# Recurrent layers on one core: Pool's B products in pairs of 1024 columns in a ring of eight, C products split as before, the gated y written in place

## What is computed

```python
xc, z = split(x @ in_w.T)                      # 512 inner channels each
u  = silu(causal_conv4(xc) + cb)
dt, Bm, Cm = split(u @ xp_w.T)                 # rank 16, state 16, state 16
dt = softplus(dt @ dt_w.T + dt_b)
A  = -exp(A_log)
def step(h, inp):                              # over tokens
    dt_t, B_t, C_t, u_t = inp
    h = exp(dt_t[:, :, None] * A) * h + (dt_t * u_t)[:, :, None] * B_t[:, None, :]
    y = einsum('bdn,bn->bd', h, C_t)
y = (ys + u * Dskip) * silu(z)
h = layer_norm(y @ out_w.T) ; x = h + residual
```

## Time and profile before

| what | value |
|---|---|
| median of 3 runs | 9465.37 us (9464.44 to 9467.9) |
| profiled execution, its own time | 9470.18 us |
| span of that execution, first to last instruction | 9468.5 us |
| mean granted PE clock | 0.949 of full speed |
| busy, share of the span | PE 87%, PEld 50%, DVE 88%, ACT 60%, POOL 54% |
| first scan, last scan (their starts) | 4538.3 us, 8777.1 us |

### The profile page before, as it was taken

How to read it: one execution, slowest core, us unless ns; L and a number is a source line. 1 busy time by engine, 2 the same in 40 slices (tenths; PEclk the granted TensorE clock), 3 DMA queues, 4 the chain that set the end, 5 groups by cost and what they waited for, 6 DMA issues and landing times. The chain is left out here.

```text
span 9468.5 us, 173659 instructions
## 1 busy us (share of the span) xinstructions
PE 8233.9 (87%) x48392; PEld 4721.2 (50%) x48392; DVE 8331.3 (88%) x12866; ACT 5642.4 (60%) x9235; POOL 5082.2 (54%) x4769
## 2 busy tenths in 40 slices
PE   6699999999999997897888888887788888888699
PEld 2366666666666666564333333333233333333466
DVE  5788888888888887997899999999699999999899
ACT  2377777777777775332666666665456656555333
POOL 1100000000000000785899999999699999999687
PEclk8799999999999999998999999999899999998899
DMA  7988888888888888111122111221222222211111
GB/s 236 306 272 281 282 280 283 281 281 279 282 283 281 280 280 267 46 43 47 77 82 82 72 56 77 82 82 44 94 80 72 76 91 91 91 68 71 53 43 40
DMA packets 1173912, 1447.40 MB, mean 153 GB/s; under 512 B 83402, under 2 KB 1053658, under 8 KB 1140736
## 3 DMA queue, kind: packets, MB, share of 16 engines
q1 hardware_dynamic: 1173568, 1444.18, 46.3%
HBM read 880.81 MB, written 564.60 MB: 153 GB/s over the span
## 5 line engine op out<-in xcount | busy, mean ns | idle before, releaser
L2109 POOL TENSOR_TENSOR mb_bx<-mb_dtu,mb_bc 128x512 f32<-128x512 f32 x2048 | 2662.0, 1324 | 13.7 <-DVE mb_hs L2209 13.2
L2352 PE MATMUL mb_y_ps<-mb_g,ident 128*128 128x512 f32 x4096 | 2187.1, 640 | 469.2 <-POOL mb_g L2116 235.0
L2396 ACT ACTIVATE mb_dA<-mb_dt,mb_a_neg 128x512 f32<-128x512 f32 x2048 | 1401.0, 688 | 1627.6 <-DVE mb_hs L2209 1084.9
L1471 POOL MEMSET f_magic<- 128x1 f32 x2 | 0.2, 98 | 3383.6 <-POOLq L127 3383.6
L2352 PEld LDWEIGHTS mb_y_ps<-mb_g,ident 128*128 128x128 f32 x4096 | 763.6, 199 | 1650.5 <-issue 729.0
L1017 ACT ACTIVATE at_tab<-at_e_ps 128x384 f32<-128x384 f32 x2064 | 1012.1, 490 | 790.1 <-PE at_e_ps L934 789.4
L1071 DVE TENSOR_REDUCE at_nmax<-at_s_ps 128x1 f32<-128x1024 f32 x1025 | 1255.2, 1225 | 35.1
L950 PE MATMUL at_pT_ps<-ident,at_probs 128*128 128x128 f32 x8192 | 1115.6, 279 | 101.8 <-ACT at_probs L1022 84.8
L1022 ACT ACTIVATE at_probs<-at_s_ps,at_nmax 128x1024 f32<-128x1024 f32 x1025 | 1140.8, 1113 | 62.5 <-DVE at_nmax L1071 39.0
L950 PEld LDWEIGHTS at_pT_ps<-ident,at_probs 128*128 128x128 f32 x8192 | 894.6, 141 | 403.2 <-ACT at_probs L1022 374.4
L2169 DVE TENSOR_TENSOR mb_g<-mb_hs,mb_bc 128x512 f32<-128x512 f32 x1472 | 993.7, 675 | 39.6 <-PE mb_y_ps L2352 38.3
(11 more groups left out here) (244 smaller groups left out, 14167.9 us busy)
## 6 DMA issues: line engine op xcount, KB each, us to landing
at_tables<-at_tab SPq DMA_DIRECT2D x1032, 384.0 KB, 4.0
at_skew<-at_tables SPq DMA_DIRECT2D x1030, 256.0 KB, 3.1
mb_bc<-mb_bc_rows SPq DMA_DIRECT2D x256, 1024.0 KB, 6.3
at_skew<-at_tables SPq DMA_DIRECT2D x773, 128.0 KB, 3.5
at_opnd<-at_q_st SPq DMA_DIRECT2D x130, 210.0 KB, 4.4
at_opnd<-at_kl_st SPq DMA_DIRECT2D x130, 210.0 KB, 4.7
at_opnd<-at_kr_st SPq DMA_DIRECT2D x130, 210.0 KB, 4.6
at_q_st<-st_parts SPq DMA_DIRECT2D x96, 256.0 KB, 4.1
```

The lines of the kernel that those rows point to most:

```text
L2109: pool.tensor_tensor(bx[:, s % RINGS, :], dtu[:, c, :], bc[:, 0, n, :], ALU.mult).then_inc(s_bx, 1)
L2352: nc.tensor.matmul(y_ps[:, c % 2, :], ident[:, :], g[:, s1 % RINGS, :], start=False, stop=(n == STATE - 1)).then_inc(s_y, 1)
L2396: nc.scalar.activation(dA[:, s % DA_RING, :], dt[:, c, :], ACT.Exp, scale=a_neg[:, c, n:n + 1]).then_inc(s_dA, 1)
```

## The change

Both rings had the length RINGS = 4. Now bx has BX_RING = 8 and g keeps G_RING = 4. Pool makes the products bx of slots s and s+1 in one instruction of 128 x 1024 at every even s: dtu of the chunk is read twice by a broadcast over the pair, and two neighbouring B rows lie side by side in bc. It waits until scan s-7 is done (the later of the two buffers that it writes) and then raises the semaphore by two, so that scan s and scan s+1 are released together. Nothing else of Pool's list moves: the 18 slots whose g Pool makes are the same, and so are the slots of all other steps.

The tile yz is gone. combine writes its product back to sz, over the gate that it reads, and the output projection reads sz of the item's parity. Two waits go with it: combine's for the output projection of the item before is removed, and ACT's first z copy at slot 46, which waited for the four combines of the item of the same parity, now waits until that item's output projection is done.

```diff
-RINGS = 4
+BX_RING, G_RING = 8, 4
...
-        bx = sb("bx", [P, RINGS, BANK])
-        g = sb("g", [P, RINGS, BANK])
+        bx = sb("bx", [P, BX_RING, BANK])
+        g = sb("g", [P, G_RING, BANK])
         carry = sb("carry", [P, SLOTS])
-        yz = sb("yz", [P, IC, BANK])
...
-                        ge(pool, s_scan, k.n * SLOTS + s - RINGS + 1)
-                        pool.tensor_tensor(bx[:, s % RINGS, :], dtu[:, c, :], bc[:, 0, n, :], ALU.mult).then_inc(s_bx, 1)
+                        if n % 2 == 0:
+                            r = s % BX_RING
+                            ge(pool, s_scan, k.n * SLOTS + s - BX_RING + 2)
+                            pool.tensor_tensor(bx[:, r:r + 2, :], dtu[:, c:c + 1, :].to_broadcast([P, 2, BANK]),
+                                               bc[:, 0, n:n + 2, :], ALU.mult).then_inc(s_bx, 2)
...
-                ge(dve, s_o, t.n * QT)
-                nc.vector.tensor_tensor(yz[:, c, :], y_ps[:, c % 2, :], sz[:, t.u, c, :], ALU.mult).then_inc(s_yz, 1)
+                nc.vector.tensor_tensor(sz[:, t.u, c, :], y_ps[:, c % 2, :], sz[:, t.u, c, :], ALU.mult).then_inc(s_yz, 1)
...
-                        nc.vector.tensor_tensor_scan(state(s), dA[:, s % DA_RING, :], bx[:, s % RINGS, :],
+                        nc.vector.tensor_tensor_scan(state(s), dA[:, s % DA_RING, :], bx[:, s % BX_RING, :],
...
-                            mm = nc.tensor.matmul(ring[:, ring_bank("out", i, k, -1), 0:D], yz[:, c, i * P:(i + 1) * P],
+                            mm = nc.tensor.matmul(ring[:, ring_bank("out", i, k, -1), 0:D], sz[:, b.u, c, i * P:(i + 1) * P],
...
-                            ge(act, s_yz, k.n * IC)
+                            ge(act, s_o, k.n * QT)
```

More of the change, by code:

```diff
@@ L2114, in body @@
                             pool.wait_ge(s_scan, m1 + 1)
-                            ge(pool, s_y, m1 - RINGS + 1)
-                            pool.tensor_tensor(g[:, s1 % RINGS, :], state(s1), bc[:, 1, s1 % STATE, :],
+                            ge(pool, s_y, m1 - G_RING + 1)
+                            pool.tensor_tensor(g[:, s1 % G_RING, :], state(s1), bc[:, 1, s1 % STATE, :],
                                                ALU.mult).then_inc(s_gp, 1)
@@ L2167, in times_c @@
                 if s1 not in TIMES_C_POOL:
-                    ge(dve, s_y, m - RINGS + 1)
-                    nc.vector.tensor_tensor(g[:, s1 % RINGS, :], state(s1), bc[:, 1, n, :], ALU.mult).then_inc(s_g, 1)
+                    ge(dve, s_y, m - G_RING + 1)
+                    nc.vector.tensor_tensor(g[:, s1 % G_RING, :], state(s1), bc[:, 1, n, :], ALU.mult).then_inc(s_g, 1)
             def combine(t, c):
@@ L2351, in body @@
                             pe.wait_ge(s_g, t.n * TC_DVE + slots_before(s1 + 1, False))
-                        nc.tensor.matmul(y_ps[:, c % 2, :], ident[:, :], g[:, s1 % RINGS, :],
+                        nc.tensor.matmul(y_ps[:, c % 2, :], ident[:, :], g[:, s1 % G_RING, :],
                                          start=False, stop=(n == STATE - 1)).then_inc(s_y, 1)
```

## The result

The changed kernel is slower: 9555.15 us (median of 4 runs, 9548.18 to 9556.81) against 9464.91 us (4 runs, 9463.94 to 9467.9) for the kernel before on the same chip. The ratio is 1.009, its 95% interval 1.0077 to 1.0103. 9482 was predicted, with 9415 to 9540 as the range, so the time lies 15 us above the range's upper end. A loss of 17 us was forecast, 90 us were measured.

What follows compares the result with a forecast made beforehand. DVE and Pool were taken as even bounds, 95% busy each; only DVE's wait for bx could be gained. Later scans and pairs met cost 0.6 us an item, 19 us over 32 items: about 9484 us, taken as 9482, range 9415 to 9540.

Steps and rivals of the forecast that it cites:

- The pair's price: Pool's bx: a 1024-column pair takes 2.30 us where two singles took 2.45, saving 4.6 us an item of Pool's work.
- no cheaper than two: Rival: a pair takes 2.45 us like two singles; late pairs at slots 26, 44, 48 cost 3.6 us an item, 9580; chance 0.07.
- Slots 44 to 48: First layer: ln product meets pair 46, +1.1 us, ln sum gives 0.5 back, scan 48 waits behind residual sum; DVE stands +0.9.
- The walk: One item followed slot by slot, noting how much later (+) DVE stands: 0.6 us an item, 19 us in all; chance 0.48.
- Slot 44: v at slot 40 ends some 0.4 us sooner; scan 44 begins 4.8 us after v's end, not 5.2: DVE stands at -0.8.
- Slots 58 to 62: v meets pair 60 and 61, waiting 1.9 us for 1.1; src * mod meets pair 62 or g 60: DVE at +1.8 in all.
- Slot 0: DVE's wait of 1.11 us for bx 0 is gone since Pool now leads: DVE stands at +0.65.
- The second layer: Product with mod meets pair 50, DVE at +1.5; at slot 62 a wait of 1.16 us goes, +0.55 at the end.
- Waits for PE: DVE's wait for PE, 1.2 us an item in the first layer, taken as not touched by the change.
- The waits go: Rival: DVE's waits for bx vanish and nothing replaces them; 9425 with half the 78 us, 9387 with all; chance 0.28.
- a bound of 0.8%: Most that could be gained: DVE's whole wait for bx, 2.7 and 2.2 us an item by layer, 78 us over 32 items.
- DVE meets a whole pair at most places: Rival: DVE's eight two-SBUF-input instructions an item can each wait 1.1 us more; 9590, or 9535 with half; chance 0.17.

Runs made afterwards that it cites:

- With lead: Changed kernel with each pair of bx products issued by Pool one slot earlier: 9399.51 us against 9471.21 for the kernel before, ratio 0.9925.
- the run with the steps moved: Changed kernel with Pool's first-layer residual sum and four output norm steps one slot later, each behind a pair: 9547.13 us, ratio 1.0077 to before.
- With lead and three pairs split: Changed kernel with pairs issued one slot earlier, those at slots 46, 48 and 0 made as two single products: 9383.69 us, ratio 0.9906 to before.
- the products in twos: Changed kernel with each pair made by two 512-column instructions, only the second raising the semaphore, by two: 9537.9 us, ratio 1.0073 to before.
- singles and lead: Changed kernel with single 512-column products in the ring of eight, each issued one slot earlier: 9430.67 us, ratio 0.9958 to before.

## Why the prediction had the sign right and the size wrong

**What bounds the kernel: right.** DVE and Pool are both near 95%, and Pool's rate is not what DVE waits for in the old order. Taking 5.8 us of work an item off Pool gave nothing by itself. With lead, pairs gave 0.3%.

**The pair's price: right.** A pair takes 2.35 and 2.34 us in the timeline of after, 2.30 from the one at 5687.85 to the next instruction; 2.30 was taken. The operand that is read twice costs nothing to be seen. The rival "no cheaper than two" is out. The Trainium skill's 2.6 cycles an element (GPSIMD Engine Reference, Performance versus the Vector engine) would give 1.11 us for 512 columns more, as an estimate; after's rows give 2.34 - 1.27 = 1.07.

**The in-place product and its waits at nothing: right**, shown by the run with singles in a ring of eight (0.9996). That the longer ring takes 1 us an item off the second layer was not seen.

**Slot 26 and slot 30: near.** 0 and +0.4 were forecast, +0.3 and another +0.4 measured. The wait at slot 26 is 0.86 for 0.70 us.

**Slots 44 to 48: right as a step, from the wrong level.** The walk let DVE lose 1.7 us here (from -0.8 to +0.9) and it lost 1.6 in the first layer (+1.1 to +2.8). Its parts came as they were told: the ln product 1.64 to 2.73, the ln sum 0.5 back, scan 48 released by a pair behind the sum.

**Slot 44: wrong, and this is the step that failed most.** The walk put DVE at -0.8 there, and it stood at +1.1: 1.9 us an item too low in the first layer, 1.8 in the second (+1.0). v took less, as forecast: 1.66 us for 2.53. But the walk had it end 0.4 us sooner than before, and it ended 0.2 later (scan 41 in the table), as DVE came to it 1.1 us late. Some 0.5 of that is DVE's g of slots 36 and 37 waiting for PE: the table has +0.5 from slot 37 to slot 38, where the walk had nothing. The larger error lies behind v. "Then dt, dtu and the pair follow" with 4.8 us from v's end to scan 44; measured are 5690.30 - 5684.11 = 6.2. I had let dt follow v's end at once. But g 39 stands between e and dt, as it did before, and now comes later: the pair ahead of it is 1.1 us longer than bx 42, and e itself had to wait 1.43 us for ACT's lnp. So v ended in the middle of g 39 and dt began 1.1 us later. Before, with v sitting out g 39, dt began 5658.68 - 5658.51 = 0.2 us after it. The earlier end of v was no gain, because the instruction that it no longer waited for now stood in dt's way. That g 39 did it is shown by the run that moves it: 5.3 us instead of 6.2. The same run shows that this delay is not what makes the kernel slow by itself: with it gone v meets the whole of pair 42, and nothing is won.

**Slots 58 to 62: near.** +0.9 was forecast for slots 58 to 62; v went from 1.67 to 2.62 as told, the src product fell from 2232 to 1569 ns, which was not, and the src sum rose by 1.1, for it meets pair 0. In the table DVE goes from +2.8 to +3.7, so the sum of +0.9 was met, but by luck: in the walk the src sum's 1.1 stood nowhere, and the src product gives back what it takes.

**Slot 0: wrong.** The walk took 1.11 us off each item for a wait that was to vanish. That wait is in the item that I followed and not in the next, whose scans of slots 0 and 1 stand together in before's timeline without one:

```profile
5840.08 2.33 DVE L2209 TENSOR_TENSOR_SCAN mb_hs<-mb_dA,mb_bx 128x512 f32<-128x512 f32 x2
```

It occurs in every second item, so at most 0.5 us an item could be had, and in after it is still there, 0.86 us at 5738.91. Measured is -0.2 from slot 63 to slot 0. This is 0.9 us an item. One item stood for two kinds of item.

**The second layer: sign right, size wrong by the same step.** +1.5 at slot 48 was forecast and is +3.0, of which slot 44 makes 1.8. Its product with mod did meet a pair, as told: the median over the layer is 2172 ns. At its end +0.55 was forecast and +1.4 measured, and the 1.4 holds a gain of 1.1 from the longer ring; the pairs alone cost 2.4.

**Waits for PE: counted at nothing, and not nothing.** They grew from 1.2 to 2.1 us an item in the first layer. The run with the steps moved shows one way in which they arise: PE has its own long steps ahead of the adding up, made slower by the low clock after it stood for late g, and DVE's ring of four for g is then full.

**Added up, first layer:** slot 44 and slot 0 account for 1.9 + 0.9 = 2.8 of the 3.7 - 0.65 = 3.1 us an item that the sum fell short, and the way from slot 0 to slot 10 (+0.2, counted at nothing) for most of the rest. Both errors point the same way. This tells where DVE stood later than in the walk, not what the kernel would have gained with that place mended. The sign of the forecast was right, but at odds that it gave itself of 0.46 for a loss above 0.2%, and with a loss a fifth of the real one.

**The rivals.** "The waits go" is out for this order: they doubled. They do go with lead, and then it is worth 0.75% with a bound of 0.8%. The bound is looser than it looks: it was read from one row and leaves out the 4.4 us of the scans into SBUF, and it takes DVE's work as fixed. With lead and three pairs split, the five groups fall from 14.2 to 13.2 us an item and the gain is 86 us, above the 78. "DVE meets a whole pair at most places" came true at three of the eight (ln product, v of slot 58, src sum; in the second layer at the mod product), and the time lies within its 9535 to 9590, but not for its reason: the five groups together cost only 0.75 us an item more than before, since v and the others give back what the ln product and the src sum take. The Trainium skill's rule (SBUF — State Buffer, Terms) that the loser at the shared port blocks for the other's full instruction fits these rows: each pair met in place of a single costs 1.1 us (the ln product's 2729 against 1642 and 1649 ns). It does not tell which instruction DVE meets, nor that v can sit out the next ones too, for which see the last section. That late release, without any long product, gives 0.7% is shown by the products in twos; that lateness and not the lock carries most of the loss is shown from the other side by the pairs with lead, which lose more at the lock (15.8 us an item for 15.0) and win 0.75%.

**What stays open.** In after the granted clock of PE was lower, 0.90 of 2.4 GHz in the first layer's stretch for 0.95, a mixture of its two levels, and PE's busy time for the same matmuls rose from 1342.44 to 1393.77 us. How much of DVE's wait for PE comes from this clock and how much from late g was not parted by any run. The rows point to both. With singles and lead DVE waits 21.5 us for PE in 12 items, nearly after's 25.0, at a clock of 0.94 and with PE busy for 1338.84 us, no more than before. But the projection at slot 47, during which nothing is added up, was slower in after: its 96 matmuls in 12 items took 66.57 us, before 58.93, with pairs and lead 46.09. With products in twos they took 58.35, as before, and the wait for PE was 11.8 us, though the mean clock of the stretch was 0.93: that mean does not tell at which matmuls the clock was low.

## What to carry to other kernels

Joining two instructions of an engine saves its fixed part (0.15 us here), but the first element's consumer waits for both, and this is paid wherever the producer is late: look for each place where the product stands behind a wait, and move the product ahead of it first. Here moving it one slot gained 0.4%, and only then did joining gain another 0.3%. When walking an item, walk one of each kind, and after each duration that gets shorter ask which instruction now stands in the place of the one that was waited for. Two runs here took away a wait that was plain to see and gained next to nothing: without g 39 v sat out the pair, and with the residual's sum out of the way DVE ran into PE's projection. So before mending one wait, look at what the engine meets next.
